# Normalised tiles of five layer norms inside attention: made by ScalarE in place of VectorE

## The reference

```python
def _layernorm(x, axis=-1, eps=1e-05):
    m = jnp.mean(x, axis=axis, keepdims=True)
    v = jnp.var(x, axis=axis, keepdims=True)
    return (x - m) / jnp.sqrt(v + eps)
...
x = x + _L0_attn_ref(_layernorm(x), Wq, Wk, Wv, Wo)       # 16 heads; scores squared, causal, divided by their sum
x = x + _L0_xattn_ref(ctx_1024, _layernorm(x))            # distances 77 x 1024, least-cost path (DTW), rows of ctx added along it
x = x + _L0_ffn_ref(_layernorm(x), ...)                   # 256 -> 1024 -> gelu -> 1024 -> 256, with butterfly factors folded in
```

## Time and profile before

| | |
|---|---|
| median of 3 executions | 914.62 us (914.38 to 915.73) |
| profiled execution, its own time | 919.23 us |
| its span in the profile | 917.5 us |
| mean granted clock of TensorE | 0.927 of full |
| attention, about | 60 to 616 us of the span |

### The profile page before, as it was taken

How to read it: one execution, slowest core, us unless ns; L and a number is a source line. 1 busy time by engine, 2 the same in 40 slices (tenths; PEclk the granted TensorE clock), 3 DMA queues, 4 the chain that set the end, 5 groups by cost and what they waited for, 6 DMA issues and landing times.

```text
span 917.5 us, 12051 instructions
## 1 busy us (share of the span) xinstructions
PE 782.3 (85%) x3927; PEld 384.2 (42%) x3927; DVE 489.3 (53%) x1921; ACT 446.9 (49%) x672; POOL 147.5 (16%) x332
## 2 busy tenths in 40 slices
PE   4887988799899978899988978867899972699998
PEld 3352323234333324333233322334476561457657
DVE  5637553531546122569997884239759886431000
ACT  1245776766667754778865757523412300241220
POOL 2121222221221111212222202101001000100100
PEclk9899997889999989979999989977999986799999
DMA  4481532210323220314422211101010012000001
GB/s 145 146 251 65 184 108 77 69 48 23 116 70 149 71 59 20 89 34 137 132 90 84 61 39 34 25 9 28 15 38 31 15 45 64 10 0 24 24 0 46
DMA packets 52761, 61.25 MB, mean 67 GB/s; under 512 B 21007, under 2 KB 31939, under 8 KB 52699
## 3 DMA queue, kind: packets, MB, share of 16 engines
q1 hardware_dynamic: 51611, 56.28, 20.4%
q0 software_dynamic: 1088, 4.19, 1.4%
HBM read 37.16 MB, written 23.30 MB: 66 GB/s over the span
## 4 chain that ended last, share of the span: by engine, by line
PE 57%; DVE 29%; ACT 6%; issue 5%; DMA 2%; SPq 1%; DVEq 0%; ACTq 0%
PE psO L1205 11%; PE psS L1188 10%; PE psS L1352 8%; PE psW L1362 7%; PE psW L1257 5%; DVE FOLD L917 3%; DVE STATS L1032 3%; PE psW L1248 3%; PE psW L1280 3%; ACT ARENA L778 3%; DVE FOLD L977 3%; PE psW L1264 2%; PE psW L1289 2%; DVE XX L1053 2%; PE psW L1292 2%
## 5 line engine op out<-in xcount | busy, mean ns | idle before, releaser
L778 ACT ACTIVATE ARENA<-psS 128x1024 f32<-128x1024 f32 (+3 forms) x384 | 301.0, 811 | 110.5 <-PE psS L1188 107.7
L1188 PE MATMUL psS<-ARENA 96*128 96x512 bf16 (+3 forms) x768 | 196.2, 347 | 30.5 <-ACT ARENA L778 29.5
L702 POOL TENSOR_SCALAR_AFFINE_SELECT ARENA<-ARENA 128x256 f32<-128x256 f32 x256 | 110.4, 435 | 410.3 <-ACT ARENA L778 408.6
L1205 PE MATMUL psO<-ARENA 128*32 128x512 f32 (+3 forms) x1536 | 173.2, 525 | 3.4 <-ACT ARENA L783 2.5
L1188 PEld LDWEIGHTS psS<-ARENA 96*128 96x128 bf16 x768 | 57.1, 100 | 219.3 <-ACT ARENA L778 125.7
L1362 PE MATMUL psW<-W2E,ARENA 128*128 128x256 f32 x512 | 114.6, 385 | 6.8 <-DVE ARENA L1168 6.2
L1362 PEld LDWEIGHTS psW<-W2E,ARENA 128*128 128x128 f32 x512 | 98.7, 193 | 23.0 <-DVE ARENA L1168 6.6
L845 ACT ACTIVATE ARENA<-psS,BEFF 128x512 f32<-128x512 f32 x64 | 43.5, 687 | 122.7 <-PE psS L1352 122.7
L1248 PE MATMUL psW<-IDENT,XX 128*128 128x128 f32 x192 | 36.9, 348 | 46.8 <-DVE XX L1053 46.8
L1080 DVE TENSOR_TENSOR X<-X,psW 128x512 f32<-128x512 f32 x32 | 21.7, 684 | 100.6 <-PE psW L1280 50.6
L1257 PE MATMUL psW<-XX,ARENA 128*128 128x512 f32 x128 | 68.0, 638 | 5.1 <-DVE ARENA L1068 3.1
(11 more groups left out here) (143 smaller groups left out, 817.9 us busy)
## 6 DMA issues: line engine op xcount, KB each, us to landing
ARENA<-qk_parts SPq DMA_DIRECT2D x192, 128.0 KB, 2.7
qk_parts<-ARENA SPq DMA_DIRECT2D x16, 768.0 KB, 3.7
out<-ARENA SPq DMA_DIRECT2D x16, 256.0 KB, 2.1
X<-in_x POOLq DMA_DIRECT2D x3, 1024.0 KB, 7.2
dist<-ARENA SPq DMA_DIRECT2D x1, 2560.0 KB, 8.1
MORE<-dist SPq DMA_DIRECT2D x16, 160.0 KB, 2.3
path<-MORE SPq DMA_DIRECT2D x16, 80.0 KB, 2.0
path<-FOLD SPq DMA_DIRECT2D x16, 80.0 KB, 2.2
```

The costliest lines, as they stand in the source:

```text
L702: pool.affine_select(out=blk, in_=blk, compare_op=ALU.is_ge, fill=0.0, base=0, pattern=[[0, 2], [1, P]], channel_multiplier=-1).then_inc(s ...
L778: nc.scalar.activation(A[:, (2 * G + a) % A_PAIRS, :, 0:N], psS[:, a, :, 0:N], ACT.Square).then_inc(s_sq, 1)
L1188: ins = nc.tensor.matmul(psS[:, a, j, 0:N], KST[0:STACK, g % 2, 2 * a + j, kt * P:(kt + 1) * P], QST[0:STACK, g % 2, 2 * a + j, q0:q0 + N] ...
L1205: ins = nc.tensor.matmul(psO[32 * j:32 * j + 32, o % 2, q0 - qc * HALF:q0 - qc * HALF + N], V1[:, kt, GH * g + j], A[:, (2 * G + j // 2) % ...
```

## The change

For the five norms listed above (x 1, 2, 3 and student 0, 2) the 40 tiles of `normal` are computed by ACT as one activation each: Identity(x * scale + bias), with scale = `RS` and bias = `SHIFT` = -mean * rstd, both one number for each partition. DVE computes `SHIFT` (128x8) with one more instruction behind the reciprocal. ACT waits for it (`s_shift`), and PE's turns of these norms wait for ACT (`s_xn_scalar`) in place of DVE. The other seven norms stay on DVE. The wait that guards `XN` is now by pairs of tiles (`turned`): the turns of the norm before that read the same half of `XN`. DVE waits before it overwrites `RS` and `SHIFT` until ACT has read them. The plan itself is the same.

```diff
+    def by_scalar(kind, b):
+        return (kind, b) in (("x", 1), ("x", 2), ("x", 3), ("student", 0), ("student", 2))
...
-    def last_turn(kind, b):
-        return max((u for u in plan if u[0] == turn_of[kind] and u[1] == b), key=plan.index)
+    def turned(kind, b, i):
+        of_pair = tiles_of[i]
+        k = of_pair.index(("normal", kind, b, i))
+        return max(ready(turn_of[of_pair[k - 1][1]], of_pair[k - 1][2], i // 2 * 2 + x) for x in range(2)) if k else 0
...
@@ scalar @@
+                elif kind == "normal" and by_scalar(*u[1:3]):
+                    _, what, b, i = u
+                    if turned(*u[1:]) and i % 2 == 0:
+                        act.wait_ge(s_ready, turned(*u[1:]))
+                    act.wait_ge(s_shift, scaled_of[what, b, 0] // (TT // 2) + 1)
+                    for t in (2 * i, 2 * i + 1):
+                        ins = nc.scalar.activation(XN[:, t], X[:, b, t], ACT.Identity, scale=RS[:, t:t + 1], bias=SHIFT[:, t:t + 1])
+                    ins.then_inc(s_xn_scalar, 1)
...
@@ vector @@
                 elif kind == "rstd":
+                    scaled_ahead = sum(plan.index(v) < plan.index(u) for v in scaled)
+                    if scaled_ahead and not by_scalar(what, b):
+                        dve.wait_ge(s_xn_scalar, scaled_ahead)
                     dve.wait_ge(s_sd, norm_of[u[1:]] + 1)
+                    if by_scalar(what, b) and scaled_of[what, b, 0]:
+                        dve.wait_ge(s_xn_scalar, scaled_of[what, b, 0])
                     vec(nc.vector.reciprocal(RS[:, t0:t1], SD[:, t0:t1]))
                     settled()
-                elif kind == "normal":
+                    if by_scalar(what, b):
+                        nc.vector.scalar_tensor_tensor(out=SHIFT[:], in0=MV[:, :, 0], scalar=-1.0, in1=RS[:],
+                                                       op0=ALU.mult, op1=ALU.mult).then_inc(s_shift, 1)
+                elif kind == "normal" and not by_scalar(*u[1:3]):
-                    if order and order % 4 == 0:
-                        dve.wait_ge(s_ready, ready(*last_turn(*normals[order - 1][1:3])))
+                    if turned(*u[1:]) and i % 2 == 0:
+                        dve.wait_ge(s_ready, turned(*u[1:]))
...
@@ tensor, turns @@
-                    pe.wait_ge(s_xn, normal_of[what, b, 2 * h + 1] + 1)
+                    if by_scalar(what, b):
+                        pe.wait_ge(s_xn_scalar, scaled_of[what, b, 2 * h + 1] + 1)
+                    else:
+                        pe.wait_ge(s_xn, normal_of[what, b, 2 * h + 1] + 1)
```

More of the change, by code:

```diff
@@ L234, in layer @@
     item_of = {u: k for k, u in enumerate(u for u in plan if u[0] in ITEM_KINDS)}
-    normals = [u for u in plan if u[0] == "normal"]
+    def by_scalar(kind, b):
+        return (kind, b) in (("x", 1), ("x", 2), ("x", 3), ("student", 0), ("student", 2))
+    every_normal = [u for u in plan if u[0] == "normal"]
+    scaled = [u for u in every_normal if by_scalar(*u[1:3])]
+    scaled_of = {u[1:]: k for k, u in enumerate(scaled)}
+    normals = [u for u in every_normal if not by_scalar(*u[1:3])]
     normal_of = {u[1:]: k for k, u in enumerate(normals)}
+    tiles_of = {k: [u for u in every_normal if u[3] == k] for k in range(TT // 2)}
     turn_of = {"x": "turn_x", "student": "turn_s", "ffn": "turn_f"}
@@ L308, in layer @@
         RS = sb("RS", [P, TT])
+        SHIFT = sb("SHIFT", [P, TT])
         CORNER = sb("CORNER", [LANES, 1])
@@ L423, in layer @@
         s_xn = sem("s_xn")
+        s_shift = sem("s_shift")
+        s_xn_scalar = sem("s_xn_scalar")
         s_part1 = sem("s_part1")
@@ L1043, in _ @@
                     _, what, b, t0, t1 = u
+                    scaled_ahead = sum(plan.index(v) < plan.index(u) for v in scaled)
+                    if scaled_ahead and not by_scalar(what, b):
+                        dve.wait_ge(s_xn_scalar, scaled_ahead)
                     dve.wait_ge(s_sd, norm_of[u[1:]] + 1)
+                    if by_scalar(what, b) and scaled_of[what, b, 0]:
+                        dve.wait_ge(s_xn_scalar, scaled_of[what, b, 0])
                     vec(nc.vector.reciprocal(RS[:, t0:t1], SD[:, t0:t1]))
                     settled()
-                elif kind == "normal":
+                    if by_scalar(what, b):
+                        nc.vector.scalar_tensor_tensor(out=SHIFT[:], in0=MV[:, :, 0], scalar=-1.0, in1=RS[:],
+                                                       op0=ALU.mult, op1=ALU.mult).then_inc(s_shift, 1)
+                elif kind == "normal" and not by_scalar(*u[1:3]):
                     _, what, b, i = u
-                    order = normal_of[u[1:]]
-                    if order and order % 4 == 0:
-                        dve.wait_ge(s_ready, ready(*last_turn(*normals[order - 1][1:3])))
+                    if turned(*u[1:]) and i % 2 == 0:
+                        dve.wait_ge(s_ready, turned(*u[1:]))
                     for t in (2 * i, 2 * i + 1):
```

## The result

The changed kernel takes 935.6 us (median of 4 runs, 934.82 to 936.66) beside 914.5 for the kernel before in the same comparison: a ratio of 1.0214, interval 1.017 to 1.0258, so 19.6 us more (15.5 to 23.6). In a second comparison it was 932.79 beside 916.24, ratio 1.0187 (1.0137 to 1.0237), 17.1 us more. The forecast was 929, or 14.5 more, with 921 to 936 as its range: 935.6 lies just inside its upper end.

The account below looks back on a forecast made before the run. PE was taken as nearly full (85% busy) and tied to ACT's squares through psS, ACT's idle time lying in crumbs. Delays of 12.7 us plus 1.8 for the clock gave 14.5, so 914.62 + 14.5 = 929.1 us; range 921 to 936.

Parts of the forecast that it names:

- absorbing rival: ACT's 107.7 us of waiting for PE takes the 19.6 added; delays halve or vanish, 915 to 921 us; chance 0.12.
- price of a tile: One Identity tile on ACT: 0.59 us alone, 0.49 in a row; 19.6 us for 40 tiles, bounds 16 to 24.
- that rival: Table loads for Identity and back to Square in each of the five norms: 12.8 us more, 942; chance 0.02.
- x 1: Normals 1 to 3 stand between step 9's second square and turn 0's copy on ACT; delay 2.5 us.
- x 2: Normal 0 pushes a square by 0.4 us; normals 1 to 3 stand before a full ACT; delay 2.9 us.
- student 0: Six tiles before step 34's squares, two before the copies for turns 0 and 1; dist's first half 3.2 us later.
- x 3: Four tiles delay step 17's first square by 2.0 us; normals 2 and 3 fit ACT's waits; delay 1.8 us.
- student 2: ACT waits 5.2 us for the late SHIFT; turn 0 starts 2.1 us later, normal 3 adds 0.2; delay 2.3 us.
- sum of delays: The five moved norms' delays to PE's awaited events add to 12.7 us, and nothing takes it back later.
- The clock: New PE gaps at student 0, x 2 and x 3 may bring half-clock stretches: 1.8 us taken, bounds 0 and 6.8.
- rival of the other side: VectorE was the limit under the path search; its 5.6 us back in x 3 and student 2 gives 909; chance 0.03.
- signs named in advance: Profile after: 40 ACT tiles of 0.59 us, SHIFT wait about 5, PE's square and copy waits up about 13 us.

Follow-up runs that it names:

- doubled run: Changed kernel with each of the 40 ScalarE activations made twice, the first into a scratch tile; 952.3 us, ratio 1.0421 to the kernel before.
- run with the gaps filled: Changed kernel with 67 more transposes on TensorE, results unread, ahead of its waits at x 1, x 2 and student 0; 930.65 us, ratio 1.0156 to the kernel before.
- spread pair: Changed kernel and kernel before, both with the planner's size of a normal at 12 instead of 3, spreading tile pairs one to a step; 904.71 and 894.6 us.

## Why the prediction was right, and where its size was off

**What bounds, and ScalarE's room.** Right: ScalarE's idle time did not take the tiles. The doubled run shows it plainest. The absorbing rival (0.12) is refuted. One reading overstates the tie, though: the 125.7 us behind ACT's squares are idle time of PE's weight loads, which overlap its matmuls; PE's own wait for squares was 29.5 us.

**The price of a tile.** Right: 592 ns alone and 0.49 us in a row, stated as 0.59 and 0.49. No table load came, so that rival fell as well; the Trainium skill ("ScalarE: Activation LUTs", "Table sets: the hidden batching unit") had said that identity is in every set, and the eight loads of before and after agree.

**The delays, norm by norm**, from the timelines, each counted from an event ahead of the norm to the first that waits for it (the clock's part within that stretch is in it):

- x 1: stated 2.5. The scores of step 9 came at 84.63 against 85.82 before, the first qk at 94.44 in both: 1.2. In the trace before PE had a gap of its own and a slow stretch here (clock 0.89 in the earlier trace rows) that the changed kernel's did not have, so the pair understates it.
- x 2: stated 2.9. Scores 16 at 241.12 against 242.36, qk at 255.18 against 251.94: 4.5. The clock of 0.68 against 0.89 is in it.
- student 0: stated 3.2. Dist at 302.53 against 296.15, less the 3.24 that it was already late at x 2's qk: 3.1. Behind it came what I had not put there, the slow dist of 3.34 for 1.93 us.
- x 3: stated 1.8. Scores 16 at 398.15 against 389.91, turn 0 at 408.52 against 398.81: 1.5.
- student 2: stated 2.1 to turn 0. 12.7 us from the scores of step 25 against 10.6: 2.1. ScalarE waited 5.4 us for `SHIFT` (stated 5.2), and the run with student 2 alone gave 2.8. What I had put at nothing behind turn 0 was the slower PE: batch 3 lost 6.2 to 6.9 us, 2.1 to 2.3 idle and 3.9 to 4.8 busy.

**The sum of delays.** Stated 12.7 us. From step 7 of batch 0 on, PE's idle time rose by 8.6 to 11.6 us, two traces of the changed kernel against those of the kernel before and of the one with no norm moved. By batch, against all traces in which it has no star, idle time rose by 0.2 to 3.2 us in batch 0 (stated 2.5), 4.5 to 5.0 in batch 1 (6.1 for the two norms), 1.0 to 1.6 in batch 2 (1.8) and 2.1 to 2.3 in batch 3 (2.3). So this part of the mechanism was right norm by norm and a little too large.

**The clock.** This is the term that was mis-sized: stated 1.8, bounds 0 and 6.8; measured 6.7 to 9.5 us of PE's busy time from step 7 on. I took one gap in three to bring a slow stretch, and of the four in the upper bound the text names three. The extra busy time is in two places: 5.0 to 5.8 us in batch 1 and 3.9 to 4.8 in batch 3, none clear of the wander in batches 0 and 2. The run with the gaps filled shows that in batch 1 the gaps brought it; the spread pair has the change without extra busy time, though its plan differs in more than the blocks. That the term recurs within 0.2 us in a second execution is against my treating it as a matter of chance.

**The range, and luck.** The bounds given for the range, 3.5 us for a slower tile and 5.0 for the clock's upper bound, lead from 929.1 to 937.6 if both are added, not to 936. That 935.6 lies inside 936 is in part luck: the clock cost about 5 to 8 us more than taken, the delays 1 to 4 less, and the two errors offset each other.

**VectorE's gain.** Stated as nothing, apart from student 2; the rival of the other side (0.03) is refuted, with no place in the trace where PE waits less for VectorE but the one that turned into a wait for ScalarE.

**The signs named in advance.** PE's waits for squares and copies were to grow by about 13 us. Squares grew by 6.5; with the 5.7 for ScalarE's tiles, a wait that I had not listed, most of the 13 is there, under two names.

What stays open: x 1's and x 3's own cost, which the table bounds at -1.7 to 2.5 and 0.6 to 3.6 us and no run has alone; why x 2 with student 0, and student 2, cost 2 to 3 us more in the changed kernel than each alone (149.3 against 147.3, 136.2 against 133.3), most of it busy time, that is slower matmuls rather than longer waits; and what the 10 us that the spread tiles still cost consist of.

## What to carry to other kernels

An engine's idle share says nothing of whether it can take a block of work: compare the block, in one piece, with the single gaps between the instructions that another engine waits for. If work must go to such an engine, put it in pieces of one gap each; here an edit that did this, and moved other work with it, halved the cost, and the same edit without the move gained 22.5 us. When PE is the bound, a new gap can cost twice, once by its length and once by slower matmuls behind it. Read both from the trace, as idle and as busy time of the same instructions, and cut the stretches so that each holds one change and begins behind the noise of the start.

## What the runs showed of the hardware

- Behind new gaps of 1.0 to 2.2 us TensorE's matmuls got slower. In the batch with x 2 and student 0 the same matmuls were busy 5.0 to 5.8 us longer beside 4.5 to 5.0 us more idle time, at a mean granted clock of 0.93 where it had been 0.96 to 0.98, and this repeated within 0.1 us in a second execution. 49 useless transposes in that batch's gaps took the extra busy time away and brought the clock to 0.98; 4.6 of the 10 us went with it.
- ScalarE's Identity with scale and bias by partition, 128x256 in fp32 from SBUF: 592 ns alone, 0.49 us from start to start. VectorE's tile in the same kernel was 0.35.
- The start of attention wandered between 54 and 60 us from run to run (55.33 and 59.89 in two executions of the same changed kernel). An early start was not kept: the scores of step 7 started at 79.83 and 81.46 in these two. So the stretch from the first square has this in it too, and a stretch that begins at step 7 leaves it out.
